# Gate scores of a mixer + expert layer: one accumulated float32 product, or four in the column quarters of the array

## What is computed

```python
xn = _layernorm(x, axis=-1)
scores = xf @ gate_w.T                 # xf = xn as (8192, 512), gate_w (8, 512)
scores = (jnp.tanh(scores) + 1.0) * 0.5
vals, idx = jax.lax.top_k(scores.T, k) # k = 1024 rows for each expert
```

## Time and profile before

| | |
|---|---|
| median of three runs | 2635.19 us |
| the profiled execution's own time | 2637.41 us |
| its span | 2635.5 us |
| gate stage (until the first mixer product) | 109.01 us |
| TensorE busy over the span | 2606.3 us, 99% |
| VectorE, ScalarE, GpSimd busy | 79%, 56%, 26% |

### The profile page before, as it was taken

How to read it: one execution, slowest core, us unless ns; L and a number is a source line. 1 busy time by engine, 2 the same in 40 slices (tenths; PEclk the granted TensorE clock), 3 DMA queues, 4 the chain that set the end, 5 groups by cost and what they waited for, 6 DMA issues and landing times.

```text
span 2635.5 us, 38833 instructions
## 1 busy us (share of the span) xinstructions
PE 2606.3 (99%) x11592; PEld 2112.6 (80%) x11592; DVE 2079.5 (79%) x3570; ACT 1481.2 (56%) x2536; POOL 675.0 (26%) x1006
## 2 busy tenths in 40 slices
PE   8999999999999999999999999999999999999998
PEld 4588888888888888888888888888888888888886
DVE  8778888888888888887877778878788787887754
ACT  5744545555455656655544555565555655556553
POOL 5422222222222222213533213223132231312101
PEclk9999999999999999999999999999999999999999
DMA  9733222233333222335447436364363643636313
GB/s 367 265 128 111 76 92 87 89 104 112 112 112 112 79 85 85 96 104 166 136 125 195 109 117 161 92 155 127 117 160 93 153 131 115 159 92 156 98 56 72
DMA packets 262638, 329.62 MB, mean 125 GB/s; under 512 B 142032, under 2 KB 142160, under 8 KB 258640
## 3 DMA queue, kind: packets, MB, share of 16 engines
q1 hardware_dynamic: 228816, 230.91, 28.2%
q0 software_dynamic: 33664, 96.75, 14.9%
HBM read 259.14 MB, written 68.45 MB: 124 GB/s over the span
## 4 chain that ended last, share of the span: by engine, by line
PE 85%; DVE 10%; issue 2%; ACT 1%; DMA 1%; SPq 0%; POOL 0%; DVEq 0%; POOLq 0%; ACTq 0%
PE ring L1584 9%; PE ring L1585 9%; PE ring L1586 9%; PE po L2564 5%; PE po L2565 5%; PE po L2566 5%; PE po L1622 4%; PE pb L2565 4%; PE pb L2566 4%; PE pb L2564 4%; PE po L1623 4%; PE po L1624 4%; PE pc L2565 2%; PE pc L2566 2%; PE pc L2564 2%
## 5 line engine op out<-in xcount | busy, mean ns | idle before, releaser
L1584 PE MATMUL ring<-xt_h,w_h 128*128 128x512 f32 x1024 | 400.1, 391 | 0.1
L2564 PE MATMUL po<-w2h,hid_h 128*128 128x512 f32 x1024 | 399.3, 390 | 0.8
L1585 PE MATMUL ring<-xt_l,w_h 128*128 128x512 f32 x1024 | 398.5, 389 | 0.0
L2565 PE MATMUL po<-w2l,hid_h 128*128 128x512 f32 x1024 | 398.5, 389 | 0.0
L1586 PE MATMUL ring<-xt_h,w_l 128*128 128x512 f32 x1024 | 398.4, 389 | 0.0
L1373 DVE SCALAR_TENSOR_TENSOR u<-xin,cw,u 128x512 f32<-128x512 f32 x384 | 288.4, 751 | 75.9 <-issue 47.0
L2041 POOL DMA_INDIRECT out_dram<-res,idx_c x64 | 105.0, 1640 | 495.0 <-DVE res L2411 483.5
L2564 PEld LDWEIGHTS po<-w2h,hid_h 128*128 128x128 f32 x1024 | 192.2, 188 | 43.9 <-DVE hid_l L2401 3.8
L1584 PEld LDWEIGHTS ring<-xt_h,w_h 128*128 128x128 f32 x1024 | 192.2, 188 | 41.0 <-DVE xt_l L542 0.9
L1586 PEld LDWEIGHTS ring<-xt_h,w_l 128*128 128x128 f32 x1024 | 192.2, 188 | 40.1
L2565 PEld LDWEIGHTS po<-w2l,hid_h 128*128 128x128 f32 x1024 | 192.2, 188 | 39.6
(11 more groups left out here) (301 smaller groups left out, 6263.1 us busy)
## 6 DMA issues: line engine op xcount, KB each, us to landing
w2r<-fc_in SPq DMA_DIRECT2D x256, 256.0 KB
wo<-wo_halves POOLq DMA_DIRECT2D x120, 512.0 KB, 4.5
w1r<-fc_in SPq DMA_DIRECT2D x144, 256.0 KB
x_tail<-x_in SPq DMA_DIRECT2D x64, 256.0 KB, 2.8
out_dram<-res SPq DMA_DIRECT2D x64, 256.0 KB, 2.0
g_x<-x_in SPq DMA_DIRECT2D x15, 1024.0 KB, 8.5
xt_rows<-g_xnt SPq DMA_DIRECT2D x15, 1024.0 KB, 10.2
rows<-xt_rows SPq DMA_DIRECT2D x15, 1024.0 KB, 6.3
```

Of the source, the lines that this page charges most:

```text
L1584: pe.matmul(ring[r % 2][:, :], w_h[:, r, q], xt_h[:, k, :], start=(k == 0), stop=False)
L1585: pe.matmul(ring[r % 2][:, :], w_h[:, r, q], xt_l[:, k, :], start=False, stop=False)
L2564: pe.matmul(dst, ah, bh, start=start, stop=False, skip_group_check=more)
L2565: pe.matmul(dst, ah, bl, start=False, stop=False, skip_group_check=more)
```

## The change

The gate weights get 24 columns of zeros beside their 8, so that a slice is 128 x 32. The product of slice k then goes to the k-th quarter of the array's columns and to the PSUM partitions 32k to 32k+31, and nothing is accumulated. The copy to `g_sc_t` takes 128 partitions. A matrix `fold` of zeros and ones (128 x 8, four stacked 8 x 8 identities with zeros between) replaces the identity in `turn_scores`, whose four transposes become four plain float32 products: each turns 128 columns and sums the four parts. GpSimd writes the zeros and builds `fold` at the start. SyncE loads the weights after the zeros are written, and behind the load of block 1.

```diff
-    gw = m.sb("g_gw", [P, KD, E])
+    gw = m.sb("g_gw", [P, KD, QUAD])
+    fold = m.sb("g_fold", [P, E])
-    sc_t = m.sb("g_sc_t", [E, TB])
+    sc_t = m.sb("g_sc_t", [P, TB])
-    pst = banks[6][0:E, :]
+    pst = banks[6][:, :]
@@ turn_scores
-            last = pe.transpose(psc[:, j * E:(j + 1) * E], sc_t[:, j * P:(j + 1) * P],
-                                ident[0:E, 0:E])
+            last = pe.matmul(psc[:, j * E:(j + 1) * E], sc_t[:, j * P:(j + 1) * P], fold[:, :], start=True, stop=True)
@@ sync
-        sp.dma_start(gw[:, :, :], t["gate_w"]).then_inc(c_gw, 16)
         load_x(1, 1)
+        sp.wait_ge(c_id, 3 + 1)
+        sp.dma_start(gw[:, :, 0:E], t["gate_w"]).then_inc(c_gw, 16)
@@ gpsimd
+        pool.memset(gw[:, :, :], 0.0).then_inc(c_id, 1)
...
+        pool.tensor_tensor(fold[:, :], ident[:, 0:E], ident[:, QUAD:QUAD + E], ALU.add).then_inc(c_id, 1)
...
+        pool.tensor_tensor(fold[:, :], fold[:, :], ident[:, 2 * QUAD:2 * QUAD + E], ALU.add).then_inc(c_id, 1)
...
+        pool.tensor_tensor(fold[:, :], fold[:, :], ident[:, 3 * QUAD:3 * QUAD + E], ALU.add).then_inc(c_id, 1)
@@ tensor
-                    pe.matmul(pst, gw[:, k, :], xnt[i][:, k, :], start=(k == 0),
-                              stop=(k == KD - 1)).then_inc(c_se, 1)
+                    pe.matmul(pst[k * QUAD:(k + 1) * QUAD, :], gw[:, k, :], xnt[i][:, k, :], start=True,
+                              stop=True).then_inc(c_se, 1)
-        pe.wait_ge(c_id, 3 + 1)
+        pe.wait_ge(c_id, 7 + 1)
```

More of the change, by code:

```diff
@@ L411, in gpsimd @@
         pool.memset(half[:, :], -0.5).then_inc(c_id, 1)
-        pool.wait_ge(c_id, 2 + 1)
+        pool.memset(gw[:, :, :], 0.0).then_inc(c_id, 1)
+        pool.wait_ge(c_id, 3 + 1)
         pool.affine_select(out=ident[:, :], in_=ident[:, :], compare_op=ALU.not_equal, fill=1.0,
                            base=0, pattern=[[-1, P]], channel_multiplier=1).then_inc(c_id, 1)
+        pool.wait_ge(c_id, 4 + 1)
+        pool.tensor_tensor(fold[:, :], ident[:, 0:E], ident[:, QUAD:QUAD + E], ALU.add).then_inc(c_id, 1)
+        pool.wait_ge(c_id, 5 + 1)
+        pool.tensor_tensor(fold[:, :], fold[:, :], ident[:, 2 * QUAD:2 * QUAD + E], ALU.add).then_inc(c_id, 1)
+        pool.wait_ge(c_id, 6 + 1)
+        pool.tensor_tensor(fold[:, :], fold[:, :], ident[:, 3 * QUAD:3 * QUAD + E], ALU.add).then_inc(c_id, 1)
         def first_half():
@@ L599, in small_high @@
             else:
-                act.wait_ge(c_id, 4 + 1)
+                act.wait_ge(c_id, 8 + 1)
                 act.copy(w.wb[:, :, 0:S], staged2[:, 3, :].rearrange("p (c s) -> p c s", s=S)).then_inc(c_sh, 1)
```

## The result

Five runs of each kernel gave a median of 2664.49 us after the change (2658.49 to 2666.39) and 2635.23 before (2635.17 to 2637.68). The medians lie 29.3 us apart; the ratio is 1.0102, 95% interval 1.0091 to 1.0113. The prediction had 2637.8 us with a range that ended at 2645.5. The second rival, the clock that falls, is what happened, and in its larger form (2662 us).

What follows compares the result with a forecast made beforehand. TensorE bounds after 109 us; before that, a 5.73 us loop through the tanh beside TensorE's 5.77 us chain. Terms +0.4 + 2.1 - 0.4 + 0.5 = +2.6 us gave 2637.8 us on the median, range 2634 to 2645.5.

Steps and rivals of the forecast that it cites:

- rival 2: Gate stage: TensorE's clock falls as it idles; 2645.4 us for four of 14 blocks, 2662 for all; chance 0.13.
- The whole saving of 1.4 us or more a block becomes idle time: Gate stage: cheaper gate products lie off the path, so their saving only idles TensorE and leaves the pitch unchanged.
- The gate products: Gate stage, off the path: 3.53 us a block become about 2.2, bounds 0.88 to 3.53.
- Rival 1: Gate stage: column quarters do not overlap and TensorE's pitch is 6.27 us; 2642.5 us, chance 0.15.
- The turn: Turned scores, on the path: 0.84 us instead of 0.34, tanh at 2.96 us, loop grows 0.35 to 6.08.
- Rivals 3 and 4: Turn at 0.19 us a record, 2646 us, chance 0.06; turn hidden behind copies, loop stays 5.73, 2635.3 us, chance 0.12.
- rival 5: Gate stage: shifted tanh parts normalisation from GpSimd's weight work, loop 5.1 us; faster, 2633 us, chance 0.04.
- Blocks 2 to 15 at full clock: Gate stage: 13 pitches of 6.08 us plus 0.6 of late loads, 79.6 against 77.5; +2.1 us.
- The third limit: Gate stage: DMA at 395 GB/s, 2.25 MB a block, would bound at about 5.7 us a block.
- Block 1 to block 2: Early gate stage: turn partly at half clock delays the tanh, T(2) moves to about 26.1; +0.4 us, bounds 0 and +1.3.
- The end of the stage: Last block to mixer's start: the score copy no longer waits for gate products, first copy earlier; -0.4 us.
- The start: Start-up: zeros, fold and later gate weights delay first transposes up to 1 us, hidden by block 1; entered at nothing.

Runs made afterwards that it cites:

- experiment 7: Changed kernel plus one unused 256-column product (0.44 us) behind each block's packed gate products; 2640.12 us, ratio 1.0012.
- experiment 2: Kernel before with only the turn changed, four plain float32 products by the 8 x 8 identity replacing four transposes; 2646.59 us, ratio 1.0039.
- experiment 1: Changed kernel plus two unused full-length products (0.88 us each) behind each block's packed gate products; 2637.70 us, ratio 1.0005.
- experiment 10: Changed kernel with turn and tanh of block b-1 moved ahead of block b's transposes and copies, plus one 0.88 us filler product; 2641.95 us, ratio 1.0021.
- experiment 4: Kernel before with only the last of each block's four gate products, three left out; 2654.18 us, ratio 1.0066.
- experiment 3: Changed kernel with the turn as four transposes of the first quarter's scores, other three quarters not summed; 2637.59 us, ratio 1.0002.
- experiment 8: Changed kernel, turn by four transposes of the first quarter only, with five identity transposes ahead of each turn except the last; 2649.03 us, ratio 1.0049.

## Why the prediction was wrong, step by step

- **The step that failed: "The whole saving of 1.4 us or more a block becomes idle time".** It was entered at nothing. Idle time on TensorE isn't free when what follows it stands on the path: the next transposes do. That step costs 25.9 us (103.58 - 77.65).
- **The chance and size of rival 2.** It was seen, with its mechanism and a price for four blocks of 14 and for all, and given 0.13. The argument against it was the clock of 1.00 over 35 us. That row has TensorE busy 34.67 of 35.07 us: it says what a full TensorE gets, and nothing of an idle one. The only row of before with a gap, 2.64 us and then the half clock, was the one that bore on it; the prediction's own sum left a gap of about 6.08 - 1.90 - 0.84 - 0.88 = 2.46 us if the quarters overlap fully. "Four of 14" also left out that a slow block makes its own gap. Its price for one block (1.9 us) was nearly right for the whole block, though not for its parts: 13 x (7.97 - 5.97) = 26.0, with 5.97 = 77.65 / 13. Up to the tanh the block shown has 5.29 - 2.88 = 2.4 us more, since the transposes take 3.67 us and not 2.94.
- **The gate products: 2.2 us taken, 0.89 measured** (59.84 - 58.95 in experiment 7, from their start to the filler's). The low bound was the truth, and it lengthened the gap. Rival 1 fell; the 0.1 us that it put on each change between the full and the quartered array stood in no row, and none shows.
- **The turn: 0.84 taken**, 0.89 in the changed kernel (62.67 - 61.78), 0.98 in experiment 2. The tanh came at T + 2.88, the loop at 5.96, both once the clock is held (experiment 1). This part was right in mechanism and 0.1 us dear. Rivals 3 and 4 fell with it, and rival 5 too: the normalisation still takes 2.45 us (experiment 1).
- **Blocks 2 to 15 at full clock: +2.1 taken, +0.2 measured** (77.65 - 77.47). The loop was a little shorter, and x came in time, as the step said (waits of 0.7 us in all, 3.3 before). That experiment 1 then lands on the forecast of 2637.8 is in part luck: it also has T(2) at 24.47, 1.3 us earlier than before, because the filler held the clock in block 1.
- **The third limit was mis-sized.** The loads of 1 MB are 1024 KB of 1024 bytes, so that a block's 2.25 MB are 2.36 million bytes, and at 395 GB/s they take 5.97 us and not 5.7, an estimate from these rows. That is above both loops (5.77 and 5.73) and at the mean of the kernel before (5.96); with the clock held the DMA share is 1.00 (experiment 1) and 0.99 (experiment 10). By this estimate the stage had about nothing to gain, whatever became of the gate products. The 5.7 went again into what was expected of experiment 10.
- **Block 1 to block 2.** T(2) came at 26.88, +1.1 instead of +0.4; the step priced the half clock for the turn alone, and the transposes of block 1 took 3.68 us, not 2.94, behind a gap of 3.51 us, not 2.64.
- **The end of the stage: -0.4 taken**, 136.45 - 130.46 = 5.99 against 5.80, +0.2, the block being slow; in experiment 1, at full clock but with filler in the way, it is 108.26 - 102.12 = 6.14, +0.3. The score copy's wait went, and the mixer starts no sooner after T(15); why, no run tells.
- **The start**: TensorE's first transposes begin at 9.60 us for 8.49, and T(1) is 18.67 for 18.45. It was hidden but for these 0.2 us.
- **The last turn**: +0.5 taken and measured (0.80 us up to the next product for 0.34), of the mixer's 1.0 us; the rest isn't explained.

## What to carry to other kernels

Before work is moved off TensorE's path, write down the idle gap that it leaves and what stands behind it; if the trace has one gap of that length followed by a low clock, price every block at that clock as well as a few of them: here all were slow. A row in which an engine is always busy says nothing about what happens when it idles. To tell a clock cause from a work cause, add useless work in the gap: here a half-length product of 0.44 us brought the loss from 29 us to 4.

## What the runs showed of the hardware that I had not expected

- Four float32 products of 128 x 32 in four column quarters overlap wholly: 0.89 us a group from its start to the next product's, against 3.53. No cost of the change from the full to the quartered array shows: the turn takes 0.89 us up to the packed products (62.67 - 61.78) and 0.98 up to plain ones (experiment 2). The Trainium skill (TensorE: Matmul & The Clock Gate, Part 3: Packing small matmuls) has 2.38 times for three column tiles; for four the measurement here is 4.0.
- Removing three of four products made the kernel 0.66% slower (experiment 4).
- The same gap was followed by either level: 1.84 us by both in experiment 3, 2.2 by each in turn in experiment 8, 2.17 by full speed in experiment 7 and 1.09 by the half in experiment 4. The length of one gap doesn't decide it alone; what else does, no run isolates.
- Still open: why the clock falls in every block of the changed kernel and of experiment 4, and in about every second block of experiment 8 behind the same gap. Experiment 8 has transposes in place of the 8-column products and so differs in both at once; experiment 4 stays low without 8-column products and without added transposes.
